# Linear attention: means' differences to GpSimd, halves added by a one-operand reduce, query dots ahead of the statistics

## The chip, the cores and the metric

The kernel runs on one core of a Trainium2 chip. Its engines work side by side, each through its own instructions in order: TensorE (PE, matrix products), VectorE (DVE), ScalarE (ACT), GpSimd (POOL) and SyncE (SP), which here only issues DMAs. They wait for one another on semaphores. The metric is the device time of one execution in microseconds; lower is better.

## The reference

A decoder layer in float32, on `x` and a context of 128 sequences of 64 positions and 128 features. Three steps follow one another, each on a layer norm of `x`, each added to `x`. The change touches the first alone:

```
b, t, e = x.shape                                  # 128, 64, 128; H = 16 heads of D = 8
q = feature_map(x @ wq + bq).reshape(b, t, H, D)   # where(x > 0, x + 1, exp(x))
k = feature_map(x @ wk + bk).reshape(b, t, H, D)
v = (x @ wv + bv).reshape(b, t, H, D)
# running over t:
S = S + einsum('bhd,bhe->bhde', kt, vt);  z = z + kt
num = einsum('bhd,bhde->bhe', qt, S);     den = einsum('bhd,bhd->bh', qt, z) + 1e-6
out = (num / den) @ wo + bo
```

`x` in it is layer-normed: `(x - mean) / sqrt(var + 1e-5)` over the 128 features. The second step is a cross attention by autocorrelation (softmax over the five best lags), the third a mixture of 8 experts, two for each row.

## The kernel before, in words

The 8192 rows are 64 tiles of 128 rows, and four tiles are a group, so there are 16 groups. The attention stage runs in slots n = -3 to 17. Each engine has its own function `slot(n, i)`; slots -3 to 3 are written out, slots 4 to 11 are a hardware loop of four rounds of two slots, slots 12 to 17 are written out again. In the loop, counts for semaphores are computed in registers. The order of the instructions in a slot is written by hand and differs between engines. One slot works on several groups at once: VectorE reads the statistics of the input of group n+3 (`z`), multiplies and sums group n (`b`), and divides and adds group n-1 (`c`); GpSimd makes features and outer products of group n+1; PE and ScalarE also prepare the Gram matrices of group n-2 (`d`).

In a slot VectorE does, for each tile k of group n, `times_q` (L908: R = running sums in PSUM times q) and `sum_heads` (L918: num = sum of R over d). Between them stand `inverses` (L957), `quotients` (L963, tile `on`), `stats` of the input (L884, four `bn_stats` into `st[:, 0]`), `key_dots` (L924: zq = key sums times q), `sum_dots` (L931), `add_attention` (L971, adds to X), `stats` of the new X (into `st[:, 1]`) and `moments` (L892, L893).

`bn_stats` gives six numbers for each row: count, mean and sum of squared deviations of the even elements, then the same three of the odd ones. `moments` makes two small tensors of them: `df`, the difference of the two means, and `mv`, the sum of the means and of the squared deviations. ScalarE (`deviations`, L679 and L680) squares `df` and scales `mv` into `sq` and `me`; GpSimd adds them (L534, `ve`), takes the power -0.5 (L542, `rs`), and makes the shift `nb` (L548, L551); ScalarE normalises rows with `rs` and `nb` (L685: `xh` for the attention, `xh2` for the Gram matrices).

GpSimd's slot is `root` (L534, L542), `features` of tile 0 (L560: qk = ex + rl, two tensors in SBUF), `shifts` (L548, L551), `outer_product` of tile 0 (L569), then features and outer product of tiles 1, 2 and 3. PE's slot has the running sums of the outer products (L1366, in the profile L1351 into `run`), the projections, the key sums (bank 4), the transposes of `on`, then `wkk` times `ct` into bank 4, which waits until `key_dots` has read that bank, then the output projection, the transposes of `xh2`, the running sums of tile 3, and the Gram matrices. Matrix products of all kinds have the line of the helper `mm`, L1351, and transposes L1355.

After the last slots the stored Gram matrices come back by DMA with another layout (`w_s<-gram_d`), and the cross attention starts by summing them (L1059).

Of the kernel before, what the change touches and what calls it, by code (L numbers as in the profile page):

```python
# [9 lines left out]
ALU = mybir.AluOpType  # L10
ACT = mybir.ActivationFunctionType
AX = mybir.AxisListType
# [6 lines left out]
GT = 4  # L19
# [36 lines left out]
def need(eng, sem, count):  # L56

    if not (isinstance(count, int) and count <= 0):
        eng.wait_ge(sem, count)
# [7 lines left out]
def build(nc, x, ctx_t, ctx_r, wqkv_p, b_all, wo, wq2, wk2, wv2t, wo2, bq2, bk2, bv2, scale, w_router, w_experts,  # L67
          tri, stri, ident, iota, dest, walk, place, late_in, out):
    with ExitStack() as ctx:
        def sb(name, shape, dt=F32):  # L70
            return ctx.enter_context(nc.sbuf_tensor(name, shape, dt))

        def sem(name):
            return ctx.enter_context(nc.semaphore(name))
# [49 lines left out]
        st = sb("st", [P, 2, GT, 6])  # L124
        mv, df = ([sb(f"{n}{i}", [P, 2, GT, w]) for i in range(2)] for n, w in (("mv", 2), ("df", 1)))
# [125 lines left out]
        x_in = sems("x_in", 2)  # L251
        ct_in = sems("ct_in", 2)

        m_st, m_mv, m_sq, m_ve, m_rs, m_mr, m_nb, a_xh = (sem(n) for n in ("m_st", "m_mv", "m_sq", "m_ve", "m_rs", "m_mr", "m_nb", "a_xh"))
        a_ex = sem("a_ex")
        a_tr, a_xT, a_proj, a_pev, a_f, a_outer = (sem(n) for n in ("a_tr", "a_xT", "a_proj", "a_pev", "a_f", "a_outer"))

# [40 lines left out]
        def settle(eng):  # L298


            eng.sem_inc(settled, 1)
# [19 lines left out]
        def stage(n, i, shift):  # L321

            if i is None and not 0 <= n + shift < NG:
                return None
            return grp(n + shift, i)

        def moment_slot(n, i, shift):

            at = n + shift if i is None else 2 * i + n + shift
            if i is not None:  # L330
                return at, (n + shift) % 2, slice(0, 2)
            if not -3 <= at <= NG:
                return None
            return at, at % 2, slice(0 if at + 3 < NG else 1, 2 if at >= 1 else 1)

        def stats_before(n, i):

            if i is not None:
                return 2 * GT * (2 * i + n + 1)
            return GT * (min(n + 3, NG) + min(max(n - 1, 0), NG))  # L340
# [176 lines left out]
        def _(pool):  # L517
# [9 lines left out]
            pool.memset(used[0][:], 0.0).then_inc(s_used, 1)  # L527
            pool.wait_ge(setup, 3)

            def root(at, p, own):  # L530

                pool.wait_ge(m_sq, 2 * (at + 3) + 2)
                need(pool, m_rs, at + 3)
                nc.gpsimd.tensor_tensor(ve[:, own], sq[:, own], me[:, own], ALU.add).then_inc(m_ve, 1)  # L534
                pool.wait_ge(m_ve, at + 4)
                if isinstance(at, int):
                    need(pool, a_xh, GT * min(at + 2, NG))
                    need(pool, d_xh, GT * (at - 2))
                else:
                    pool.wait_ge(a_xh, GT * (at + 2))  # L540
                    pool.wait_ge(d_xh, GT * (at - 2))
                nc.gpsimd.tensor_tensor(rs[p][:, own], ve[:, own], power[:, own], ALU.pow).then_inc(m_rs, 1)  # L542
# [19 lines left out]
            def outer_product(g, p, r, k):  # L562
                t = GT * g + k
                pool.wait_ge(a_f, t + 1)
                pool.wait_ge(a_pev, 3 * t + 3)
                need(pool, b_run, t - GT + 1)
                kk = qk[p][:, k, E:2 * E].rearrange("p (h d) -> p h d", h=H)
                vv = v8[k % 2][:].rearrange("p (h e) -> p h e", h=H)
                nc.gpsimd.tensor_tensor(  # L569
                    outer[k].rearrange("p (h e d) -> p h e d", h=H, e=D), vv.unsqueeze(3).broadcast_to([P, H, D, D]),  # L570
                    kk.unsqueeze(2).broadcast_to([P, H, D, D]), ALU.mult).then_inc(a_outer, 1)

            def slot(n, i):
                m, a1 = moment_slot(n, i, -1), stage(n, i, 1)
                if i is None and n == -1:
                    pool.wait_ge(bias_ch, 8)
                if m:
                    root(*m)
                if a1:
                    features(*a1, 0)  # L580
                if m:
                    shifts(*m)
                if a1:
                    outer_product(*a1, 0)
                    for k in range(1, GT):
                        features(*a1, k)
                        outer_product(*a1, k)

            slots(pool, slot)

            for k in range(2):
# [59 lines left out]
        def _(act):  # L651
# [22 lines left out]

            def deviations(at, p, own):

                act.wait_ge(m_mv, 2 * (at + 3) + 2)
                need(act, m_ve, at + 3)
                nc.scalar.activation(sq[:, own], df[p][:, own, :, 0], ACT.Square, scale=0.5).then_inc(m_sq, 1)  # L679
                nc.scalar.activation(me[:, own], mv[p][:, own, :, 1], ACT.Copy, bias=LN_EPS, scale=1.0 / E).then_inc(m_sq, 1)  # L680
# [161 lines left out]
        def _(dve):  # L842
# [35 lines left out]
                step(nc.vector.scalar_tensor_tensor(bias3[0:3, :], bias_p[2][:], id_s[0:3, 2:3], bias_r, ALU.mult, ALU.add))  # L878

            def stats(g, at, h):  # L880
                need(dve, m_mv, 2 * (at + 3))
                settle(dve)
                for k in range(GT):
                    nc.vector.bn_stats(st[:, h, k, :], X[:, bass.ds(GT * g + k, 1), :].rearrange("p a b -> p (a b)")  # L884
                                       ).then_inc(m_st, 1)

            def moments(at, p, own, seen):

                dve.wait_ge(m_st, seen)
                need(dve, m_mr, at + 2)  # L890
                settle(dve)
                nc.vector.tensor_tensor(df[p][:, own, :, 0], st[:, own, :, 1], st[:, own, :, 4], ALU.subtract).then_inc(m_mv, 1)  # L892
                nc.vector.tensor_tensor(mv[p][:, own], st[:, own, :, 1:3], st[:, own, :, 4:6], ALU.add).then_inc(m_mv, 1)  # L893

            def stats_e(g):
                need(dve, e_mv, GT * g)
# [24 lines left out]
            def key_dots(g, p, r):  # L921

                dve.wait_ge(b_keys, g + 1)
                nc.vector.tensor_tensor(  # L924
                    zq[:].rearrange("p (k c x) -> p c k x", k=GT, c=2), bank[4][:].rearrange("p (c k x) -> p c k x", c=2, k=GT),
                    qk[p][:, :, 0:E].rearrange("p k (c x) -> p c k x", c=2), ALU.mult).then_inc(b_dots, 1)
# [32 lines left out]
            def quotients(g, p, r):  # L959
                dve.wait_ge(c_rden, g + 1)  # L960
                need(dve, c_tr, g)
                dve.wait_ge(b_red, GT * g + GT)
                nc.vector.tensor_tensor(  # L963
                    on[:].rearrange("p t (h d) -> p (t h) d", h=H), num[p][:].rearrange("p t (h d) -> p (t h) d", h=H),
                    rden.unsqueeze(2).broadcast_to([P, GT * H, D]), ALU.mult).then_inc(c_on, 1)
# [8 lines left out]
            def slot(n, i):  # L974
                z, b, c, m = *(stage(n, i, k) for k in (3, 0, -1)), moment_slot(n, i, 0)
                if b:
                    times_q(*b, 0)
                    sum_heads(*b, 0)
                if c:
                    if i is None and c[0] == 0:  # L980
                        dve.wait_ge(kk_w, 1)
                    inverses(*c)
                if b:
                    times_q(*b, 1)
                if c:
                    quotients(*c)
                if z:
                    g, p, r = z
                    dve.wait_ge(x_in[p], 16 * r + 16)
                    stats(g, m[0], 0)  # L990
                if b:
                    key_dots(*b)
                if m and not c:
                    moments(*m, stats_before(n + 1, i))
                if b:
                    sum_heads(*b, 1)
                    sum_dots(*b)
                if i is None and n == -3:
                    fold_projection()
                    split_biases()  # L1000
                if i is None and n == -1:
                    dve.wait_ge(w_in, N_W)
                    nc.vector.tensor_copy(bv2_wide[:], bv2_s[:, 0:1].broadcast_to([P, P])).then_inc(fold_wide, 1)
                    fold_queries()
                if i is None and n == NG:
                    split_fold()
                if b:
                    times_q(*b, 2)
                    sum_heads(*b, 2)
                if c:  # L1010
                    add_attention(*c)
                if b:
                    times_q(*b, 3)
                if c:
                    dve.wait_ge(c_x1, c[0] + 1)
                    stats(c[0], m[0], 1)
                if b:
                    sum_heads(*b, 3)
                if c:
                    moments(*m, stats_before(n + 1, i))  # L1020
# [27 lines left out]
            n = 0  # L1048
# [146 lines left out]
            n = 0  # L1195
# [29 lines left out]
            for b in range(NT // NSORT):  # L1225
                own = slice(b * NSORT, (b + 1) * NSORT)
# [537 lines left out]
```

## Time and profile before

| | us |
|---|---|
| three timed runs | 618.99, 619.33, 620.18; median 619.33 |
| the profiled execution | 620.77 |
| its span, first to last instruction | 619.0 |
| the eight slots of the hardware loop (79.81 to 195.84) | 116.03 |
| VectorE busy in them | 114.61 |
| PE busy in them | 109.15 |
| GpSimd busy in them | 102.64 |
| ScalarE busy in them | 83.87 |
| ScalarE's waits for PE ahead of L664, nine slots | 10.8 |
| busy over the whole span: PE, VectorE, GpSimd, ScalarE | 554.9 (90%), 503.6 (81%), 410.3 (66%), 395.7 (64%) |

The attention stage takes the first 260 us or so of the span. Busy time counts an instruction from its start to its end, also the part in which it stands still. Instructions of one engine can overlap a little: the next one starts while the last one drains, so the time that an instruction takes from its engine is read from its start to the start of the next. An idle time in brackets behind a row names what ended it.

### The profile page before, as it was taken

What the parts mean: (1) busy time and instruction counts of PE and PEld (TensorE: products, weight loads), DVE (VectorE), ACT (ScalarE), POOL (GpSimd) and SP (SyncE); (2) the same over time, 40 slices, a digit from 0 to 9 for tenths busy, and PEclk for the clock granted to TensorE, in tenths of its full rate; (3) what the DMA queues carried; (4) which work ended last, traced back from release to release, by engine and by line L of the source; (5) the groups of instructions that cost most, each with busy time, mean ns of one, the idle gap of its engine ahead of it and who ended that gap; (6) DMA issues with size and microseconds to landing.
All of it is one profiled execution on the core that took longest, in us unless ns stands there. A gap on an engine that the chain in (4) does not pass through costs nothing.

```text
span 619.0 us, 16196 instructions
## 1 busy us (share of the span) xinstructions
PE 554.9 (90%) x4286; PEld 410.2 (66%) x4287; DVE 503.6 (81%) x1416; ACT 395.7 (64%) x1070; POOL 410.3 (66%) x475
## 2 busy tenths in 40 slices
PE   2888999999999998787998868999999999999993
PEld 1343444444444454465997535899999999999993
DVE  4499999999999999765487898466887878877883
ACT  3556777767666775423877412445888888878882
POOL 2999888888888985204876402764576766757762
PEclk9999999999999998989899887999999999999997
DMA  5510111111161111832566570221111111111110
GB/s 154 176 64 1 35 36 35 34 47 46 43 102 35 35 35 34 123 105 70 171 189 171 101 115 10 60 46 38 37 50 50 48 49 48 52 39 48 52 45 23
DMA packets 49976, 41.03 MB, mean 66 GB/s; under 512 B 21971, under 2 KB 40278, under 8 KB 49926
## 3 DMA queue, kind: packets, MB, share of 16 engines
q1 hardware_dynamic: 44150, 29.68, 19.8%
q0 software_dynamic: 4960, 10.49, 6.6%
q8 instruction: 23, 0.38, 0.3%
q10 hardware_dynamic: 816, 0.26, 0.2%
q14 instruction: 27, 0.22, 0.1%
HBM read 27.54 MB, written 12.88 MB: 65 GB/s over the span
## 4 chain that ended last, share of the span: by engine, by line
PE 54%; DVE 16%; issue 14%; DMA 5%; ACT 5%; POOL 4%; DVEq 1%; SPq 1%; POOLq 0%; ACTq 0%
PE bank L1351 28%; PE run L1351 22%; DVE st L884 3%; DVE R L908 3%; PE run L1618 2%; DMA w_s<-gram_d 2%; PE bank L1355 2%; ACT xs L788 2%; POOL qk L560 1%; DVE mean_early L1059 1%; DMA ct<-in_ctx_r 1%; ACT xh L685 1%; PE run L1542 1%; POOL shared L569 1%; DVE zq L924 1%
## 5 line engine op out<-in xcount | busy, mean ns | idle before, releaser
L569 POOL TENSOR_TENSOR shared<-v,qk 128x1024 f32<-128x1024 f32 x64 | 125.0, 1953 | 7.5 <-POOL qk L560 5.7
L624 POOL DMA_INDIRECT shared<-xs_d,row_u x91 | 87.7, 963 | 62.3 <-DVE row_u L1249 31.3
L631 POOL DMA_INDIRECT out_x<-shared x64 | 63.6, 994 | 47.6 <-DVE shared L1321 20.8
L908 DVE TENSOR_TENSOR R<-run,qk 128x1024 f32<-128x1024 f32 x64 | 77.7, 1215 | 10.5 <-PE run L1351 9.9
L918 DVE TENSOR_REDUCE num<-R 128x128 f32<-128x1024 f32 x64 | 77.7, 1213 | 1.5
L1351 PE MATMUL bank<-wqkv,xT 128*64 128x128 f32 (+1 forms) x384 | 69.9, 350 | 5.2 <-ACT v L667 4.5
L1351 PEld LDWEIGHTS bank<-wqkv,xT 128*64 128x64 f32 (+1 forms) x384 | 33.1, 158 | 59.0 <-issue 30.1
L1351 PE MATMUL run<-shared,tris_s 64*64 64x512 f32 x512 | 70.6, 622 | 0.1
L817 ACT ACTIVATE shared<-run,scale_s 128x128 f32<-128x128 f32 (+1 forms) x78 | 30.1, 386 | 41.2 <-PE run L1618 41.2
L685 ACT ACTIVATE xh<-X,nb,rs 128x128 f32 (+1 forms) x126 | 52.0, 502 | 4.4 <-POOL nb L551 4.4
L560 POOL TENSOR_TENSOR qk<-ex,rl 128x256 f32<-128x256 f32 x64 | 46.6, 728 | 9.1 <-ACT ex L669 6.9
L1351 PE MATMUL run<-w_s,hid 128*128 (+1 forms) x312 | 41.4, 275 | 0.0
L1351 PE MATMUL bank<-w_s,hid 128*128 (+1 forms) x308 | 41.0, 276 | 0.0
L821 ACT ACTIVATE ct<-w_s 128x512 f32 x64 | 39.7, 621 | 0.2 <-issue 0.2
L664 ACT ACTIVATE ex<-bank 128x256 f32<-128x256 f32 x64 | 24.5, 383 | 23.4 <-PE bank L1351 23.2
L706 ACT ACTIVATE oT<-bank 128x512 f32<-128x512 f32 x16 | 9.6, 597 | 46.7 <-PE bank L1355 46.7
L1342 DVE TENSOR_TENSOR hid<-run,shared 128x256 f32<-128x256 f32 x78 | 33.0, 423 | 7.6 <-ACT shared L827 7.4
L1351 PEld LDWEIGHTS run<-w_s,hid 128*128 128x128 f32 x312 | 38.1, 192 | 0.1
L1351 PEld LDWEIGHTS bank<-w_s,hid 128*128 128x128 f32 x308 | 37.6, 192 | 0.4 <-DVE hid L1342 0.2
L827 ACT ACTIVATE shared<-run 128x256 f32<-128x256 f32 x78 | 30.0, 385 | 11.1 <-PE run L1351 8.1
L827 ACT ACTIVATE shared<-bank 128x256 f32<-128x256 f32 x77 | 29.7, 386 | 10.5 <-PE bank L1351 8.2
L1342 DVE TENSOR_TENSOR hid<-bank,shared 128x256 f32<-128x256 f32 x77 | 32.5, 422 | 2.2 <-ACT shared L827 1.7
(271 smaller groups left out, 1417.0 us busy)
## 6 DMA issues: line engine op xcount, KB each, us to landing
xs_d<-xs SPq DMA_DIRECT2D x16, 270.0 KB, 5.4
X<-in_x SPq DMA_DIRECT2D x16, 256.0 KB, 2.8
ct<-in_ctx_t SPq DMA_DIRECT2D x16, 256.0 KB, 2.9
ct<-in_ctx_r SPq DMA_DIRECT2D x16, 256.0 KB, 3.7
gram_d<-gd SPq DMA_DIRECT2D x14, 256.0 KB, 2.4
w_s<-in_w_experts SPq DMA_DIRECT2D x8, 384.0 KB, 3.9
circ<-prob_d SPq DMA_DIRECT2D x30, 64.0 KB, 2.8
shared<-xs_d,row_u POOLq DMA_INDIRECT x91, 2.6
```

The source lines that it names most:

```text
L560: nc.gpsimd.tensor_tensor(qk[p][:, k, :], ex[k % 2][:], rl[k % 2][:], ALU.add).then_inc(a_f, 1)
L569: nc.gpsimd.tensor_tensor(outer[k].rearrange("p (h e d) -> p h e d", h=H, e=D), vv.unsqueeze(3).broadcast_to([P, H, D, D]), kk.unsqueeze(2 ...
L624: nc.gpsimd.indirect_dma_start(xg[q], None, xs_d[:, :], bass.IndirectOffsetOnAxis(ap=rows, axis=0)).then_inc(xg_in[q], 16)
L631: nc.gpsimd.indirect_dma_start(out[:, :], bass.IndirectOffsetOnAxis(ap=xg[(NXI + j) % NX][:, DEST:DEST + 1].bitcast(U32), axis=0), yg[q], ...
L685: nc.scalar.activation(dst[:, k, :], X[:, bass.ds(GT * g + k, 1), :].rearrange("p a b -> p (a b)"), ACT.Identity, bias=nb[p][:, h, k:k + 1 ...
L817: nc.scalar.activation(xgT[p][:, cols], bank[0][:, cols], ACT.Copy, scale=scale_s[:, 0:1]).then_inc(x_xT, 1)
L821: nc.scalar.activation(w_tile[n % 2][0], w_s[:, dyn(held[0] * W_E, 2 * HID)], ACT.Copy).then_inc(x_wa, 1)
L827: nc.scalar.activation(silu[p][h], bank[1 + 2 * p + h][:, HID:2 * HID], ACT.Silu).then_inc(x_silu, 2 // len(items_of(i, up[0])))
L908: nc.vector.tensor_tensor(R[:, 0:D * E].rearrange("p (h e d) -> p h e d", h=H, e=D), run[k % 2][:].rearrange("p (h e d) -> p h e d", h=H, ...
L918: nc.vector.tensor_reduce(num[p][:, k, :], R[:, 0:D * E].rearrange("p (x d) -> p x d", d=D), AX.X, ALU.add).then_inc(b_red, 1)
L1342: nc.vector.tensor_tensor(hid[p][h][:], bank[1 + 2 * p + h][:, 0:HID], silu[p][h], ALU.mult).then_inc(x_h, 2 // len(items_of(i, j)))
L1351: return nc.tensor.matmul(o, l, r, start=start, stop=stop, skip_group_check=True)
```

## The change

`df` is made on GpSimd by a new function `differences`, which stands between `features` and `outer_product` of tile 3 and signals on a new semaphore `m_df`. `mv` stays on VectorE, but is a `tensor_reduce` over the two halves of `st`, seen as the last axis: one operand of 32 elements a partition instead of two of 16. In VectorE's slot `key_dots` comes before `stats` of the input. ScalarE's `deviations` waits for `m_df` and `m_mv`, and `stats` waits for both before it writes `st` again.

```diff
+            def differences(at, p, own, seen):
+
+                pool.wait_ge(m_st, seen)
+                need(pool, m_sq, 2 * (at + 2))
+                nc.gpsimd.tensor_tensor(df[p][:, own, :, 0], st[:, own, :, 1], st[:, own, :, 4], ALU.subtract).then_inc(m_df, 1)
...
             def slot(n, i):
-                m, a1 = moment_slot(n, i, -1), stage(n, i, 1)
+                m, now, a1 = moment_slot(n, i, -1), moment_slot(n, i, 0), stage(n, i, 1)
...
                 if a1:
                     outer_product(*a1, 0)
-                    for k in range(1, GT):
+                    for k in range(1, GT - 1):
                         features(*a1, k)
                         outer_product(*a1, k)
+                    features(*a1, GT - 1)
+                if now:
+                    differences(*now, stats_before(n + 1, i))
+                if a1:
+                    outer_product(*a1, GT - 1)
...
             def deviations(at, p, own):
 
-                act.wait_ge(m_mv, 2 * (at + 3) + 2)
+                act.wait_ge(m_df, at + 4)
+                act.wait_ge(m_mv, at + 4)
                 need(act, m_ve, at + 3)
...
             def stats(g, at, h):
-                need(dve, m_mv, 2 * (at + 3))
+                need(dve, m_mv, at + 3)
+                need(dve, m_df, at + 3)
                 settle(dve)
...
-                nc.vector.tensor_tensor(df[p][:, own, :, 0], st[:, own, :, 1], st[:, own, :, 4], ALU.subtract).then_inc(m_mv, 1)
-                nc.vector.tensor_tensor(mv[p][:, own], st[:, own, :, 1:3], st[:, own, :, 4:6], ALU.add).then_inc(m_mv, 1)
+                halves = st[:, own].rearrange("p s t (h f) -> p s t f h", h=2)[:, :, :, 1:3]
+                nc.vector.tensor_reduce(mv[p][:, own], halves, AX.X, ALU.add).then_inc(m_mv, 1)
...
                 if c:
                     quotients(*c)
+                if b:
+                    key_dots(*b)
                 if z:
                     g, p, r = z
                     dve.wait_ge(x_in[p], 16 * r + 16)
                     stats(g, m[0], 0)
-                if b:
-                    key_dots(*b)
```

## Rows read from the trace of the kernel before

**Rows 1.** Windows: busy time of each engine over the loop's eight slots.
```profile
sum 116.03, PE 109.15 PEld 53.29 DVE 114.61 ACT 83.87 POOL 102.64; mean PE 13.64 PEld 6.66 DVE 14.33 ACT 10.48 POOL 12.83
```

**Rows 2.** Windows: slots 13 and 14, and the sum of slots 2, 3, 12, 13, 14.
```profile
210.21:224.38 14.17, 13.80 (x107) 6.66 (x99) 13.59 (x20) 10.31 (x33) 12.82 (x12) 1.00 0.13 39
224.38:238.12 13.74, 13.10 (x99) 6.24 (x95) 13.16 (x22) 8.64 (x28) 12.15 (x12) 1.00 0.14 39
sum 70.94, PE 65.72 PEld 32.38 DVE 69.03 ACT 49.93 POOL 63.44; mean PE 13.14 PEld 6.48 DVE 13.81 ACT 9.99 POOL 12.69
```

**Rows 3.** Timeline of VectorE in the loop: start us, us, line, operation [idle before].
```profile
156.93 0.86 DVE L884 BATCH_NORM_STATS2 st<-X 128x6 f32 x4
157.72 0.67 DVE L924 TENSOR_TENSOR zq<-bank,qk 128x512 f32<-128x512 f32 x1
...
162.41 0.68 DVE L971 TENSOR_TENSOR X<-X,bank 128x512 f32 x1
163.15 1.23 DVE L908 TENSOR_TENSOR R<-run,qk 128x1024 f32<-128x1024 f32 x1
...
166.19 0.63 DVE L892 TENSOR_TENSOR df<-st 128x8 f32<-128x8 f32 x1
166.74 0.16 DVE L893 TENSOR_TENSOR mv<-st 128x16 f32<-128x16 f32 x1
166.83 1.21 DVE L908 TENSOR_TENSOR R<-run,qk 128x1024 f32<-128x1024 f32 x1
```

**Rows 4.** Timeline of GpSimd in the loop: tile 0's features, then tile 3.
```profile
156.63 0.73 POOL L560 TENSOR_TENSOR qk<-ex,rl 128x256 f32<-128x256 f32 x1
157.31 0.20 POOL L548 TENSOR_TENSOR mr<-mv,rs 128x8 f32<-128x8 f32 x1
...
166.07 0.72 POOL L560 TENSOR_TENSOR qk<-ex,rl 128x256 f32<-128x256 f32 x1 [0.25 <-ACT ex L669]
167.02 1.95 POOL L569 TENSOR_TENSOR shared<-v,qk 128x1024 f32<-128x1024 f32 x1 [0.23 <-POOL qk L560]
```

**Rows 5.** Timeline of slot 1, VectorE and GpSimd at the moments.
```profile
50.41 0.16 DVE L892 TENSOR_TENSOR df<-st 128x8 f32<-128x8 f32 x1
50.49 0.73 DVE L893 TENSOR_TENSOR mv<-st 128x16 f32<-128x16 f32 x1
...
50.41 0.78 POOL L560 TENSOR_TENSOR qk<-ex,rl 128x256 f32<-128x256 f32 x1
```

**Rows 6.** Waits from 79 to 209 us (nine slots): us in total, times, longest.
```profile
PE bank L1351 <- DVE zq L924: 6.0, 9, 0.7
...
POOL qk L560 <- ACT ex L669: 2.7, 9, 0.5
...
POOL qk L560 <- POOL shared L569: 1.8, 9, 0.2
```

**Rows 7.** Groups of instructions in the loop: count | busy us, mean ns | idle before.
```profile
L918 DVE TENSOR_REDUCE num<-R 128x128 f32<-128x1024 f32 x32 | 38.8, 1213 | 0.9
...
L931 DVE TENSOR_REDUCE den<-zq 128x64 f32<-128x512 f32 x8 | 5.4, 676 | 0.0
```

**Rows 8.** Timeline of PE: slots of the loop, then slots 13 and 14.
```profile
161.41 0.66 PE L1355 MATMUL bank<-id_s,xh 128*128 128x128 f32 x4
...
170.43 1.09 PE L1351 MATMUL run<-shared,tris_s 64*64 64x512 f32 x8
...
214.99 0.63 PE L1355 MATMUL bank<-id_s,on 128*128 128x128 f32 x4
...
218.84 0.66 PE L1355 MATMUL bank<-id_s,xh 128*128 128x128 f32 x4 [0.24 <-ACT xh L685]
...
229.17 0.63 PE L1355 MATMUL bank<-id_s,on 128*128 128x128 f32 x4 [0.40 <-DVE on L963]
```

**Rows 9.** Timeline of VectorE at the end of the attention stage.
```profile
261.69 0.83 DVE L1043 TENSOR_SCALAR xh<-X,rs,nb 128x128 f32<-128x128 f32 x2 [1.69 <-POOL nb L551]
262.70 7.15 DVE L1059 TENSOR_REDUCE mean_early<-w_s 112x64 f32<-112x4096 f32 x1 [0.19 <-DMA w_s<-gram_d]
```

More of the change, by code:

```diff
@@ L252, in build @@
         ct_in = sems("ct_in", 2)
-        m_st, m_mv, m_sq, m_ve, m_rs, m_mr, m_nb, a_xh = (sem(n) for n in ("m_st", "m_mv", "m_sq", "m_ve", "m_rs", "m_mr", "m_nb", "a_xh"))
+        m_st, m_mv, m_df, m_sq, m_ve, m_rs, m_mr, m_nb, a_xh = (sem(n) for n in ("m_st", "m_mv", "m_df", "m_sq", "m_ve", "m_rs", "m_mr", "m_nb", "a_xh"))
         a_ex = sem("a_ex")
```

## The prediction
> **What bounds the kernel now.** I read the page first. Over the whole span no engine is full (PE is busy for 90%, VectorE for 81%), but the change sits in the attention stage only, so I cut that stage into slots with the windows view, from one product `R` of tile 0 (L908) to the next. The eight slots of the hardware loop take 116.03 us, 14.50 each, and VectorE is busy for 114.61 of them, 99% [rows 1]. The slots written out around the loop take 13.7 to 14.4 us [rows 2]. So VectorE sets the pace, but PE (109.15) and GpSimd (102.64, without its short gaps) are close behind, and what the change gives ends where one of them takes over.
>
> Busy is not the same as working. In the timeline `df` (L892), a subtraction of 8 elements per partition, lasts 0.63 us, and `mv`, which adds twice as many, 0.16 [rows 3]. GpSimd's `qk` (L560) runs from 166.07 to 166.79, and `df` ends at 166.82 [rows 4]: the end of one is the end of the other. At slot 1 `qk` runs 50.41 to 51.19; there `df` got through in 0.16 and it is `mv` that lasts 0.73, to 51.22 [rows 5]. Both are VectorE instructions with two operands in SBUF, and so is `qk` on GpSimd. The wait is not for data, it is for GpSimd's instruction to end. `R` (L908), with one operand in PSUM, runs beside GpSimd at its usual 1.21. The Trainium skill says the same in "SBUF — State Buffer", section "Who interferes with whom": a VectorE instruction with two SBUF inputs and a GpSimd instruction that reads SBUF exclude each other, and `tensor_reduce` on trn2 never takes part. This case's trace agrees on the first half (0.63 against 0.16), and on the second as far as reduces of 1024 elements go.
>
> A second wait is PE's: it waits 6.0 us in 9 slots for `zq` (L924), 0.67 each, before it multiplies `ct` by `wkk` [rows 6]. PE works in order, so that wait is handed on to the running sums of tile 3. VectorE feels its tail: `X` starts at 162.41 and ends at 163.09, and `R` of tile 3 starts only at 163.15, where `R` after `mv` starts 0.07 before `mv` ends [rows 3]. That is some 0.15 us per slot.
>
> **The change part by part, for one slot of the loop.**
>
> *`df` leaves VectorE.* From `df`'s start to `mv`'s is 0.55 us (166.19 to 166.74) [rows 3]. All of it goes: -0.55.
>
> *`mv` becomes a reduce.* It reads 32 elements instead of two operands of 16. No row shows so small a reduce; the two that there are take 1213 ns for 1024 elements and 676 ns for 512 [rows 7], which is 1.05 ns an element and 0.14 fixed, so 0.17 for 32. The ends are 0.16 (`mv` now) and 0.68 (the smaller reduce, if its time were mostly fixed, which would eat nearly all of the 0.55). I take 0.18, by the line through both rows: +0.02. If a reduce were held up by GpSimd as `mv` was, the stall would stay; the reduces of 1024 ran beside GpSimd all the time with a mean of 1213 ns [rows 7], which speaks against it.
>
> *`zq` moves ahead of the statistics.* It starts 0.79 earlier (157.72 to 156.93) and the four `bn_stats` one `zq` later, about 0.6 [rows 3]. PE's 0.67 of waiting goes, of which some 0.35 reach tile 3's sums: the transposes of `xh2` need ScalarE's normalised rows, and in slot 13, where PE doesn't wait for `zq`, it waits 0.24 for those rows instead [rows 8]. VectorE's 0.15 goes. The later statistics are read only at the end of the slot, 9 us on. No DMA is issued in the moved step, and nothing is moved past in SP's or GpSimd's queue; SP's context load follows `d_k`, which comes earlier.
>
> *`df` on GpSimd.* It stands between `qk` and `outer` of tile 3. These start 0.95 apart with `qk` 0.72 long, so 0.23 is a gap for the semaphore [rows 4]. A tensor_tensor of the same size, `mr`, starts 0.68 after its `qk` and takes 0.20 [rows 4], so `df` would be over after 0.88, inside the 0.95. The two new waits compare with register values. Their cost isn't shown by itself: at least 0, at most one more gap like the 0.23 plus `df`'s own 0.20, 0.43 in all. I take 0.03. Behind it in GpSimd's queue stand `outer` of tile 3, then `ve` and `rs` of the next slot.
>
> *ScalarE waits for both `df` and `mv`.* `df` is over some 0.1 later than now. Behind that wait is the evacuation of projection 0 (L664), and it waits for PE anyway, 10.8 us in nine slots by the waits view. If that cover were gone it would cost 0.1.
>
> *Waits before the statistics* (`m_df` beside `m_mv`): `df` will have been read behind `qk` of tile 3, at some 152.5 for the statistics at 157.5; nothing.
>
> **What is late next.** Three floors for a slot of the loop:
> - VectorE: 14.50 - 0.55 + 0.02 - 0.15 = 13.82.
> - GpSimd: of its 14.50, 2.7 + 1.8 us in 9 slots are waits ahead of `qk` for ScalarE's `ex`, which come of phase [rows 6]; that leaves 14.50 - 0.50 + 0.03 = 14.03.
> - PE and ScalarE in turn: transposes of `on` to those of the rows, 3.85 where `zq` isn't waited for (214.99 to 218.84), then from the rows' transposes to the end of tile 2's sums, 161.41 to 171.52, 10.11 [rows 8]. Sum 13.96.
>
> GpSimd has microseconds of lead over most of its readers, so 8 slots of 0.07 more than PE hardly show. I take 14.0: 0.50 saved per slot, 8 x 0.50 = 4.0.
>
> Outside the loop: slots 2, 3 and 12 take 70.94 - 14.17 - 13.74 = 43.03, 14.34 each [rows 2]; GpSimd's gaps are shorter there and VectorE's floor of 13.82 holds: 3 x 0.5 = 1.5. Slot 1 has a stall of 0.57 (0.73 against 0.16) with PE waiting: 0.6. Slot 13 has no statistics between `on` and `zq`, so the move does nothing, but its stall goes; PE waited 0.40 for the `on` that followed [rows 8], and that is what comes through: 0.4. Slot 14 is bound by PE: 0.1. At the end the last group's `df` is now a step on GpSimd between VectorE and ScalarE, 0.1 to 0.2 longer. VectorE waits 1.69 for `nb` there and then 0.19 for a DMA [rows 9], so at most 0.1 comes through. Sum: 4.0 + 1.5 + 0.6 + 0.4 + 0.1 - 0.1 = 6.5 us. Everything behind the attention hangs on its last Gram store, and I let it move up as a block.
>
> The profiled execution took 620.77 us around a span of 619.0. So the profiled one becomes 614.3 with a span of 612.5, and as the timed runs have a median of 619.33, the median becomes 612.8.
>
> **Rivals.**
> - *PE and ScalarE, or GpSimd, bind earlier* (chance 0.20). The floors are sums of single links; if the ring of PE and ScalarE keeps some of its short waits, or `df` on GpSimd costs its upper 0.43, a slot of the loop is 14.2 to 14.4. For: all three floors are within 0.2 of each other, and VectorE lost by 0.55 + 0.15 what the other two have not. Against: slot 14, bound by PE, takes 13.74. It gives 8 x 0.2 + 1.5 + 0.6 = 3.7 us: 615.6.
> - *VectorE alone sets the pace* (0.08): 8 x 0.68 instead of 4.0 makes 7.9: 611.4.
> - *The stall passes to the reduce, or the reduce is long* (0.06). Then only the 0.15 of the moved dots comes through, 1.2 us at the most, partly lost: 618.8. The 0.73 of `mv` in slot 1 shows that a stall can pass on; the 1213 of the reduces speaks against.
> - *Slower: `df` on GpSimd is held up in its turn* (0.06). Place: between `qk` and `outer` of tile 3, where VectorE now starts `R` at the very time. If GpSimd had to let `R` (1.21) end, the pair would be 0.95 + 1.0 or so apart, GpSimd's slot 14.0 + 1.0 = 15.0, against 14.50: +4.0 in the loop, less 1.1 still won outside it: 622.2. It decides from 0.5 us on per slot. Against: GpSimd's `outer` starts at 167.02 in the middle of an `R` and lasts its 1.95 [rows 3, 4]. By the same page of the Trainium skill an instruction with at most one SBUF input doesn't contend, so this would not happen; the trace agrees.
>
> **How the numbers follow.** My forecast has 0.60, with its own range 611.7 to 614.3. Less than 0.2% (1.24 us) can't be told from no change. Faster: 0.60 + 0.20 + 0.08, and a little of the fourth case, 0.89; same 0.05; slower 0.06. The range takes in the two neighbours, 611.0 to 616.4, and leaves out both the passed-on stall and the slower case.
>
> **What would show it.** The `df` group on POOL with a mean near 0.2 us, and `outer` of tile 3 still 0.95 after its `qk`. A reduce for `mv` of 0.15 to 0.2 in all its instances. PE's wait for `zq` gone; VectorE's `R` of tile 3 without a wait; VectorE's busy share in the loop below 99%, with short waits for PE or GpSimd. Slots of 14.0 us and a Gram store of the last part some 6 us earlier. A slot of 14.3 or more, with VectorE waiting for `run`, would refute the floors of PE and GpSimd; a long `mv` refutes the cause of the stall.

## The result, and the profile after

The changed kernel takes 611.85 us (median of 4 runs, 611.06 to 613.12), the kernel before in the same comparison 619.50. The ratio is 0.9878, with a 95% interval of 0.9858 to 0.9897: 7.65 us between the medians. A second comparison (`changed_again` below) gave 612.97 against 618.74, a ratio of 0.9908 (0.9881 to 0.9936), 5.8 us. The forecast was 612.8, 6.5 us below the kernel before. The profiled execution took 611.89 us around a span of 610.1.

The same windows as in [rows 1], the eight slots of the loop, now from 79.15 to 190.48 us (us of the window, busy time and instructions of PE, PEld, DVE, ACT, POOL, granted clock, DMA share, GB/s):

```profile
120.98:134.86 13.88, 13.45 (x103) 6.65 (x99) 13.79 (x22) 10.38 (x34) 12.90 (x14) 1.00 0.13 38
134.86:148.84 13.98, 13.56 (x103) 6.61 (x99) 13.78 (x23) 10.33 (x34) 12.99 (x14) 1.00 0.13 38
...
sum 111.33, PE 107.93 PEld 53.10 DVE 110.21 ACT 82.61 POOL 103.06; mean PE 13.49 PEld 6.64 DVE 13.78 ACT 10.33 POOL 12.88
```

111.33 instead of 116.03: 13.92 us a slot, 4.7 saved. VectorE's timeline in the loop of the changed kernel, to be held against [rows 3]:

```profile
139.52 0.68 DVE L937 TENSOR_TENSOR zq<-bank,qk 128x512 f32<-128x512 f32 x1
140.12 0.86 DVE L897 BATCH_NORM_STATS2 st<-X 128x6 f32 x4
...
145.00 0.68 DVE L984 TENSOR_TENSOR X<-X,bank 128x512 f32 x1
145.59 1.22 DVE L921 TENSOR_TENSOR R<-run,qk 128x1024 f32<-128x1024 f32 x1
...
148.63 0.17 DVE L906 TENSOR_REDUCE mv<-st 128x16 f32<-128x32 f32 x1
148.84 1.23 DVE L921 TENSOR_TENSOR R<-run,qk 128x1024 f32<-128x1024 f32 x1
```

The long `df` is gone and `mv` takes 0.17. `R` of tile 3 starts 0.59 after `X`, no longer 0.74. But from `mv`'s start to `R`'s it is 0.21 here, and was 0.09. GpSimd's timeline at the same place, against [rows 4]:

```profile
148.68 0.73 POOL L566 TENSOR_TENSOR qk<-ex,rl 128x256 f32<-128x256 f32 x1
149.37 0.21 POOL L534 TENSOR_TENSOR df<-st 128x8 f32<-128x8 f32 x1
149.64 1.95 POOL L575 TENSOR_TENSOR shared<-v,qk 128x1024 f32<-128x1024 f32 x1
```

`outer` starts 0.96 after its `qk`, as before with nothing between them. And the waits in nine slots, against [rows 6] (us in total, times, longest):

```profile
ACT ex L675 <- PE bank L1364: 8.7, 10, 1.0
...
PE bank L1368 <- ACT xh L697: 3.3, 9, 0.5
...
ACT sq L691 <- POOL df L534: 1.6, 7, 0.3
POOL qk L566 <- ACT ex L680: 0.7, 2, 0.4
```

PE's 6.0 us for `zq` are gone. In their place PE waits 3.3 for ScalarE's normalised rows (`xh2`, written by L697). ScalarE waits 1.6 for `df` (L691), and behind that still 8.7 for PE (L675). GpSimd's waits for `ex` fell from 2.7 to 0.7.

Where the time went, by landmarks on VectorE (starts of the first `R` of a slot, and of the first sum of the cross attention):

| stretch | before | after | difference |
|---|---|---|---|
| start to slot 0 | 24.83 | 24.67 | -0.2 |
| slot 0 | 11.91 | 13.00 | +1.1 |
| slot 1 | 14.41 | 13.79 | -0.6 |
| slots 2, 3, 12 | 43.03 | 41.48 | -1.5 |
| slots 4 to 11 (loop) | 116.03 | 111.33 | -4.7 |
| slots 13 and 14 | 27.91 | 27.37 | -0.5 |
| slot 15 to `mean_early` | 24.58 | 24.41 | -0.2 |
| up to `mean_early` | 262.70 | 256.05 | -6.65 |
| behind it, to the end of the span | 356.3 | 354.05 | -2.2 |

The last line is no effect of the change that I can show. The same code behind the attention stage took 352.8 to 357.0 us in the profiled executions of the variants below, and 355.8 in the changed kernel's second. The landmark of 256.05 came back at 256.04, but its first and last stretch scatter, too: over all traces the start of slot 0 lies at 24.26 to 24.83, and the stretch from slot 15 to `mean_early` takes 23.39 to 24.58, with 24.19 and 23.39 in two traces of one and the same kernel (`slot0_order` and `slot0_again`). What the change does is best read from slots 0 to 14 alone: 213.29 us before, 206.97 after and 207.05 in the changed kernel's second trace. That is 6.3 us.

### The profile page after: what moved, and what is told of

Same layout as the page of the kernel before. It is cut to its first block, busy times and chain, and to the rows that moved or that the text cites. A ratio compares the mean times of both kernels' runs of the same rounds, so it can differ in the third digit from the quotient of the medians.

```text
span 610.1 us, 16245 instructions
## 1 busy us (share of the span) xinstructions
PE 553.6 (91%) x4286; PEld 409.2 (67%) x4287; DVE 496.9 (81%) x1396; ACT 394.2 (65%) x1070; POOL 413.5 (68%) x495
## 4 chain that ended last, share of the span: by engine, by line
PE 44%; issue 19%; POOL 13%; DVE 11%; DMA 5%; ACT 5%; SPq 2%; POOLq 1%; DVEq 0%; ACTq 0%
PE bank L1364 21%; PE run L1364 20%; POOL shared L575 5%; POOL qk L566 4%; DMA X<-in_x 3%; ACT xs L800 2%; PE run L1631 2%; DMA shared<-xs_d,row_u 1%; SPq L420 1%; DVE mean_early L1072 1%; ACT xh L697 1%; PE run L1555 1%; DVE R L921 1%; PE bank L1368 1%; DVE st_e L911 1%
## 5 line engine op out<-in xcount | busy, mean ns | idle before, releaser
L697 ACT ACTIVATE xh<-X,nb,rs 128x128 f32 (+1 forms) x126 | 52.3, 510 | 4.5 <-POOL nb L557 4.3
L675 ACT ACTIVATE ex<-bank 128x256 f32<-128x256 f32 x64 | 24.8, 388 | 18.6 <-PE bank L1364 18.5
```

The costliest lines, as they stand in the source:

```text
L697: nc.scalar.activation(dst[:, k, :], X[:, bass.ds(GT * g + k, 1), :].rearrange("p a b -> p (a b)"), ACT.Identity, bias=nb[p][:, h, k:k + 1 ...
```

## The experiments

Each was timed in five rounds beside the kernel before, in three jobs; a number in brackets is the interval of the ratio. The table gives from each one's trace the mean loop slot, the sum of slots 0 to 14 (before 213.29, changed 206.97) and the landmark `mean_early`.

| kernel | us (before in that job) | ratio | loop slot | slots 0 to 14 | mean_early |
|---|---|---|---|---|---|
| dots_only | 620.77 (617.86) | 1.005 (1.003 to 1.0071) | 14.42 | 215.40 | 263.97 |
| dots_back | 613.80 (617.86) | 0.9941 (0.9918 to 0.9963) | 14.07 | 207.96 | 255.91 |
| two_operands | 617.23 (617.86) | 0.9992 (0.997 to 1.0013) | 13.91 | 212.23 | 261.03 |
| reduce_only | 618.55 (617.86) | 1.0012 (0.9994 to 1.0031) | 14.50 | 213.10 | 261.50 |
| slot0_order | 612.11 (617.52) | 0.9903 (0.9868 to 0.9938) | 13.92 | 205.83 | 254.36 |
| pool_extra | 612.47 (617.52) | 0.992 (0.9891 to 0.9948) | 13.92 | 206.53 | 255.02 |
| dve_extra | 613.47 (617.52) | 0.9934 (0.9908 to 0.996) | 13.99 | 208.19 | 256.26 |
| act_extra | 616.07 (617.52) | 0.9977 (0.9955 to 0.9999) | 14.19 | 210.99 | 259.79 |
| changed_again | 612.97 (618.74) | 0.9908 (0.9881 to 0.9936) | 13.92 | 207.05 | 256.04 |
| slot0_again | 610.14 (618.74) | 0.986 (0.9837 to 0.9884) | 13.91 | 206.08 | 253.90 |
| pool_larger | 612.18 (618.74) | 0.9908 (0.9872 to 0.9944) | 14.03 | 207.99 | 256.19 |

**The parts one at a time.** `dots_only`: the kernel before, with

```diff
                 if c:
                     quotients(*c)
+                if b:
+                    key_dots(*b)
                 if z:
...
-                if b:
-                    key_dots(*b)
```

> The kernel before with one edit: the dots of q stand in front of the input's statistics; df and mv stay on VectorE as two-operand instructions. Main theory (the stall comes of two SBUF operands on VectorE meeting GpSimd's qk, the move only takes PE's wait for zq away): df still lasts about 0.6 us, R of tile 3 loses its 0.15 us of waiting, a loop slot goes from 14.50 to about 14.35, and slot 0 costs 0.9 us, since zq waits there 0.7 for the key sums that the statistics covered. Together -0.5 to -1.5 us: 618 to 619. Rival (the moved dots are the main gain, because PE's wait of 0.67 per slot holds everybody): loop slots near 13.9 and 613 or less.

Slower than before by 0.5%, where 0.5 to 1.5 us less were expected. The loop slot came out at 14.42 (14.35 was expected), but slots 0 and 1 took 29.54 us (14.15 and 15.39) instead of 26.32: `df` met GpSimd's `outer` there and lasted 1.70 and 1.71 us. In the loop `R` of tile 3 does start 0.59 to 0.60 after `X`, so the 0.15 is gone, but the stall has grown by some 0.07, and it now goes to and fro. VectorE's timeline of two slots, and GpSimd's features of tile 3 beside them:

```profile
139.23 0.68 DVE L892 TENSOR_TENSOR df<-st 128x8 f32<-128x8 f32 x1
139.84 0.16 DVE L893 TENSOR_TENSOR mv<-st 128x16 f32<-128x16 f32 x1
153.67 0.16 DVE L892 TENSOR_TENSOR df<-st 128x8 f32<-128x8 f32 x1
153.75 0.74 DVE L893 TENSOR_TENSOR mv<-st 128x16 f32<-128x16 f32 x1
...
139.16 0.72 POOL L560 TENSOR_TENSOR qk<-ex,rl 128x256 f32<-128x256 f32 x1 [0.25 <-ACT ex L669]
...
153.68 0.77 POOL L560 TENSOR_TENSOR qk<-ex,rl 128x256 f32<-128x256 f32 x1 [0.25 <-ACT ex L669]
```

In the first slot `qk` has begun, and `df` waits for its end. In the second `df` is 0.01 ahead of `qk` and gets through in 0.16, `qk` is 0.05 longer than usual, and it is `mv` behind it that waits until `qk` ends. Who comes first goes first; the two slots alternate like this through the whole loop.

`reduce_only`: the kernel before with `mv` as the one-operand reduce (the two lines of the change's diff), `df` left where it was.

> The kernel before with one edit: mv is the one-operand reduce; df stays on VectorE with its two operands, the dots stay behind the statistics. Main theory: df still lasts 0.6 in the loop, mv 0.18; only slot 1, where mv had the stall, can gain 0.5 at most: 619 to 620. Rival (a lighter mv also lets df through): 615 or less.

As the main theory had it: loop slots of 14.50, `df` 0.62 to 0.63 in them, `mv` 0.15 to 0.18 everywhere, and the time that of before. In slot 1 the stall, which `mv` had before, is now on `df` (0.53), and the slot is 0.19 shorter. A light `mv` does nothing for a `df` that meets GpSimd.

`dots_back`: the changed kernel with the dots behind the statistics.

> The changed kernel with one edit undone: the dots of q stand behind the input's statistics again; df on GpSimd and the one-operand reduce stay. Main theory: no stall, PE waits for zq again. A loop slot 14.0 to 14.1, slot 0 gains 0.9 us back: 612 to 613.5, close to the changed kernel. Rival (both edits are needed together, PE's wait for zq caps the slot as soon as VectorE is faster): loop slots of 14.3 and more, 616 or more.

The loop slot is 14.07, 0.15 more than in the changed kernel. PE waits 4.4 us in nine slots for `zq`, and `R` of tile 3 again starts 0.74 after `X`. Slot 0 is 1.2 us shorter (11.83 against 13.00). Over slots 0 to 14 this kernel takes 207.96 against 206.97: the move gives back 2.2 us in the later slots, pays 1.2 of them in slot 0, and is worth 1.0 in all. That `mean_early` comes at the same time (255.91) is due to the two stretches that scatter. By the times it is 613.8 and 0.9941, and the changed kernel's two ratios are 0.9878 and 0.9908, from other jobs; I don't read a difference from that.

`two_operands`: the changed kernel with `mv` as it was,

```diff
-                halves = st[:, own].rearrange("p s t (h f) -> p s t f h", h=2)[:, :, :, 1:3]
-                nc.vector.tensor_reduce(mv[p][:, own], halves, AX.X, ALU.add).then_inc(m_mv, 1)
+                nc.vector.tensor_tensor(mv[p][:, own], st[:, own, :, 1:3], st[:, own, :, 4:6], ALU.add).then_inc(m_mv, 1)
```

> The changed kernel with one edit undone: mv is again a tensor_tensor with two SBUF operands, on VectorE; df stays on GpSimd, the dots stay in front. Main theory: mv now meets GpSimd's qk, df or outer product and lasts until it ends, 0.3 to 0.8 us in most slots instead of 0.16; the slot goes back to 14.2 to 14.5 and the time to 615 to 618. Rival (the gain is that one instruction less stands on VectorE, whatever its operands): mv 0.16 in all slots and the time that of the changed kernel, 612.

The time was in the expected range, the way there was not. In the loop `mv` takes 0.17 to 0.19 with both operands in SBUF, and the slots are as short as the changed kernel's, 13.91. The whole loss is outside it, where `mv` lasts 1.71 in slot 0, 1.76 in slot 1, 0.54 in slots 2 and 3, 0.57 and 0.70 in 12 and 13. Against the changed kernel slot 0 is 2.4 us longer, slot 1 1.6, and these four 0.2 to 0.5 each. VectorE and GpSimd in slots 0 and 1, then in the loop:

```profile
31.46 1.71 DVE L905 TENSOR_TENSOR mv<-st 128x8 f32<-128x8 f32 x1 [0.18 <-DVE st L897]
...
53.50 1.76 DVE L905 TENSOR_TENSOR mv<-st 128x16 f32<-128x16 f32 x1
...
152.87 0.17 DVE L905 TENSOR_TENSOR mv<-st 128x16 f32<-128x16 f32 x1
...
31.20 1.95 POOL L575 TENSOR_TENSOR shared<-v,qk 128x1024 f32<-128x1024 f32 x1
...
53.28 1.96 POOL L575 TENSOR_TENSOR shared<-v,qk 128x1024 f32<-128x1024 f32 x1
...
152.99 0.73 POOL L566 TENSOR_TENSOR qk<-ex,rl 128x256 f32<-128x256 f32 x1
```

31.46 + 1.71 = 33.17, and `outer` ends at 33.15; 53.50 + 1.76 = 55.26, and `outer` ends at 55.24. In the loop slot shown `mv` has started 0.12 before `qk` and is nearly through; in an earlier one it starts only 0.02 before `qk` (97.17 and 97.19) and still takes 0.17. So the reduce is worth its 5.3 us (212.23 to 206.97 over slots 0 to 14) not in the steady loop but where VectorE and GpSimd stand in another phase, that is, where the one comes to `mv` while the other is in the middle of an instruction. As a reduce `mv` takes 0.16 to 0.18 in every slot of every trace that has `df` on GpSimd, whatever the phase.

**Slot 0.** `slot0_order` and `slot0_again` are the same kernel, the changed one with the old order in slot 0:

```diff
+                early = i is None and n == 0
-                if b:
+                if b and not early:
                     key_dots(*b)
                 if z:
...
+                if b and early:
+                    key_dots(*b)
```

> The changed kernel, but in slot 0 alone the statistics stand in front of the dots of q as before. In the changed kernel zq waits 0.73 us there for the key sums and mv 0.18 for the statistics. Main theory: both waits go and the rest moves up, 0.9 us less: 611.0. Rival (another engine sets slots 0 and 1, or the time is lost again later): same as the changed kernel within 0.3.

> The changed kernel with the old order of dots and statistics in slot 0 alone, a second time, now beside the changed kernel on one chip. Its first trace had the attention stage end 1.7 us earlier than the changed kernel's. Expected: 1 to 2 us below the changed kernel; rival (lost again in the later stages): equal to it.

`changed_again` stood beside the second:

> The changed kernel itself, unedited, so that it stands beside the others on one chip. Main theory: its attention stage ends 6.6 us earlier than before, and the rest of its gain of 7.6 in the first comparison lay in the later stages, where executions differ from one another by a microsecond or two: -5.5 to -7.5 against before. Rival (the change also makes the later stages 1 us faster): -7.6 and a shorter stretch behind the attention stage again.

In the changed kernel `zq` waits in slot 0 for key sums that PE has just begun, and `mv` waits for statistics that nothing covers; with the old order both waits are gone:

```profile
29.19 0.69 DVE L937 TENSOR_TENSOR zq<-bank,qk 128x512 f32<-128x512 f32 x1 [0.73 <-PE bank L1364]
...
30.84 0.17 DVE L906 TENSOR_REDUCE mv<-st 128x8 f32<-128x16 f32 x1 [0.18 <-DVE st L897]
```

```profile
28.33 0.86 DVE L897 BATCH_NORM_STATS2 st<-X 128x6 f32<-128x128 f32 x4
29.14 0.69 DVE L937 TENSOR_TENSOR zq<-bank,qk 128x512 f32<-128x512 f32 x1
29.75 0.16 DVE L906 TENSOR_REDUCE mv<-st 128x8 f32<-128x16 f32 x1
```

(the first is the changed kernel, the second `slot0_again`). Slot 0 takes 11.84 and 12.13 us in the two traces, against 13.00 and 13.10 in the changed kernel's two and 11.91 before, and no other slot up to 14 differs by more than 0.02. Slot 0 scatters a little itself: in `pool_larger` and `dve_extra`, which leave it as it is in the changed kernel, it takes 12.79 and 12.89. So the old order is worth about 1 us there, near the 0.9 that was expected. `mean_early` comes 1.7 and 2.1 earlier, but what goes beyond 1.1 lies in the stretches that scatter. In one job the medians are 610.14 against 612.97, and 8.6 us (1.4%) below the kernel before. Of these 2.8 us only about 1 is shown to come of the edit: in its first job the same kernel had the ratio 0.9903, no better than the changed kernel's 0.9878 and 0.9908.

**What sets the slot of 13.92.** `act_extra`: one more copy on ScalarE ahead of the normalised rows `xh2`.

```diff
+                    nc.scalar.activation(dx[:], wqkv[:, 0:2 * E], ACT.Copy).then_inc(m_dx, 1)
                     norm(g, m[0], m[1], 1, xh2, d_xh, GT // 2 if i is None and g == NG - 1 else GT)
```

> The changed kernel with one more copy on ScalarE in front of the normalised rows for the Gram matrices (128x256 of a constant weight tile into a tile that nobody reads), about 0.3 us in every slot with that step (14 to 16 of them). PE waits 0.4 per slot for those rows in the changed kernel. If the ring of PE and ScalarE sets the slot: +0.25 per slot, +3 to +4 us. If VectorE or GpSimd set it with the ring 0.1 behind: +2. If ScalarE has room: within 0.3.

ScalarE in the loop:

```profile
143.71 0.44 ACT L728 ACTIVATE dx<-wqkv 128x256 f32<-128x256 f32 x1
144.02 1.65 ACT L699 ACTIVATE xh<-X,nb,rs 128x128 f32 x4
```

The copy takes 0.31 of ScalarE's time (from its start to that of `xh`), and the loop slot grows by 0.27 (113.50 for the eight). So the ring of PE and ScalarE (PE waits for ScalarE's rows, ScalarE for PE's products) stood only 0.04 below the slot of 13.92.

`dve_extra`: one more reduce on VectorE behind `mv`.

```diff
+                    nc.vector.tensor_reduce(dx[:, 0:H], wqkv[:, 0:E].rearrange("p (h d) -> p h d", h=H), AX.X, ALU.add).then_inc(m_dx, 1)
```

> The changed kernel with one more reduce on VectorE behind mv (128 elements of a constant weight tile to 16, into a tile that nobody reads, in slots 1 to 16), 0.28 us by itself, about 0.2 of VectorE's time. If VectorE sets the slot of 13.9 (its floor was forecast at 13.82, and its timeline shows no gap in the loop): +0.2 per slot, 13 or so slots, +2.5 us. If PE and ScalarE or GpSimd set it with VectorE 0.1 behind: +1.3. If VectorE has room: 0.

VectorE in the loop:

```profile
135.05 0.18 DVE L908 TENSOR_REDUCE mv<-st 128x16 f32<-128x32 f32 x1
135.14 0.28 DVE L912 TENSOR_REDUCE dx<-wqkv 128x16 f32<-128x128 f32 x1
135.34 1.22 DVE L927 TENSOR_TENSOR R<-run,qk 128x1024 f32<-128x1024 f32 x1
```

From `mv` to `R` it is 0.29, only 0.08 more than the 0.21 without the reduce, and the slot grows by 0.08 (111.95 for the eight). In the written-out slots, where it was 0.12 without, the slot grows by 0.17. Less time was added than expected, but all of it reaches the slot, so VectorE is at its floor, too.

`pool_extra` and `pool_larger` put a tensor_tensor behind `df` on GpSimd, of 8 and of 128 elements.

> The changed kernel with one more small tensor_tensor on GpSimd behind df (a sum of two constant operands of df's size into a tile that nobody reads). The gap behind qk is filled by df, so this one costs GpSimd 0.2 to 0.3 us per slot. If GpSimd is one of the engines that set the slot of 13.9: loop slots 14.1 to 14.2, +2 us in all, less in the written-out slots where GpSimd has 0.5 to spare. If it isn't: within 0.3 of the changed kernel.

> The changed kernel with a larger tensor_tensor on GpSimd behind df in slots 1 to 16 (128x128 of a constant weight tile into a tile that nobody reads), some 0.45 us, of which the gap behind qk hides nothing more. The small one tried before cost GpSimd only 0.05 per slot and moved nothing, so it could not tell. If GpSimd stands at its floor in the loop (13.9 by its own timeline): loop slots +0.35 to +0.4, 114 to 114.5 us for the eight. If it has room against PE and ScalarE, the slots grow by that much less; by 0 if it has 0.4.

```diff
+                nc.gpsimd.tensor_tensor(dx[:, own, :, 0], power[:, own], power[:, own], ALU.add).then_inc(m_dx, 1)      # pool_extra
...
+                    nc.gpsimd.tensor_tensor(dx[:, 0:E], wqkv[:, 0:E], wqkv[:, E:2 * E], ALU.add).then_inc(m_dx, 1)      # pool_larger
```

Two slots of `pool_larger` by the windows view, slot 4 and slot 9:

```profile
78.76:92.73 13.97, 13.46 (x103) 6.64 (x99) 13.78 (x22) 10.21 (x33) 13.04 (x15) 1.00 0.14 40
...
148.53:162.71 14.18, 13.32 (x103) 6.45 (x100) 13.87 (x22) 10.41 (x33) 13.26 (x15) 1.00 0.13 37
```

The small one moved `outer` by 0.05 and nothing else: no answer. The larger one moved it by 0.31. Of the eight loop slots the first four stay at 13.88 to 13.97, then come 14.07, 14.18, 14.20 and 14.09; the eight take 112.24, less than the 114 that was expected. GpSimd's `df` in the first of them shows why:

```profile
93.23 0.21 POOL L536 TENSOR_TENSOR df<-st 128x8 f32<-128x8 f32 x1
...
107.42 0.21 POOL L536 TENSOR_TENSOR df<-st 128x8 f32<-128x8 f32 x1
...
121.61 0.21 POOL L536 TENSOR_TENSOR df<-st 128x8 f32<-128x8 f32 x1
```

Here it already comes every 14.19 us, while VectorE's slots still take 13.88 and 13.97. GpSimd runs ahead of its readers, falls 0.26 behind in each slot, and only when the lead is used up does its own slot become everybody's. 14.19 less the 0.31 is 13.88, and that is, by this reckoning, GpSimd's floor in the changed kernel.

## Why the prediction was right, step by step

- *`df` leaves VectorE, -0.55, because two SBUF operands meet GpSimd.* Shown. `dots_only` and `two_operands` move the stall to `mv` and to other GpSimd instructions, and each time it ends 0.02 to 0.04 after that instruction. With `df` on GpSimd and `mv` a reduce no trace has it.
- *The reduce is never held up and costs +0.02.* Both hold: 0.16 to 0.18 in all 20, and from its start to `R`'s it is 0.10 in `reduce_only`'s loop and 0.12 in the changed kernel's written-out slots, where the sum has 0.11. What the sum lacks is another term. In the changed kernel's loop 0.21 pass until `R`, and in `two_operands`, where `mv` is no reduce, it is 0.20 to 0.22 as well: it is not the reduce. The extra reduce of `dve_extra` added only 0.08 there and not 0.2, so about 0.1 of the 0.21 is a delay of `R` that other work on VectorE can cover, as `df`'s stall did. What the loop's slots have and the written-out ones don't are counts computed in registers; that these are the cause is argued, not shown. So VectorE's floor is 13.92, not 13.82.
- *The moved dots take away 0.15 on VectorE and give PE 0.35.* In the loop, yes: `dots_back` is 0.15 slower per slot, `R` of tile 3 starts 0.74 after `X` there and 0.59 with the move, and PE now waits 0.37 for ScalarE's rows. That the 0.67 would not all come through was right.
- *`df` on GpSimd is free.* In the loop, yes: `outer` 0.96 after `qk`, was 0.95. In the written-out slots it costs 0.05 (0.85 after `qk`, was 0.80).
- *ScalarE's wait for both costs nothing.* It waits 1.6 us for `df`, and the cover is there: 8.7 us of waiting for PE behind it.
- *Floors of 13.82, 14.03 and 13.96, slot 14.0.* Measured: floors of 13.92, 13.88 and 13.88, slot 13.92. VectorE's was taken 0.1 too low, GpSimd's 0.15 and the ring's 0.1 too high. The forecast let GpSimd and PE set the slot, and it is VectorE that does. That 14.0 came so near 13.92 is in part luck: the three errors don't point the same way. 4.7 were saved, not 4.0.
- *Slots 2, 3, 12: 1.5.* Measured 1.55. *Slots 13 and 14: 0.4 + 0.1.* Measured 0.54, all of it in slot 13.
- *Slot 1: 0.6.* Measured 0.62.
- *Slot 0.* It has no term in the sum, and that is the worst error: it lost 1.1 us. I looked at the moved dots in the loop, where the key sums end 1.7 us before `zq` starts (137.79 and 139.52), and never asked in slot 0, where they are not ready. `slot0_order` and `slot0_again` show that order as the cause: with the old one slot 0 is back at 11.8 and 12.1.
- *The rest moves up as a block, at most 0.1 lost.* The stage's end moved by 6.65 where 6.5 was the sum, and slots 0 to 14 by 6.3 where it has 6.6. The nearness is partly luck: the loop gave 0.7 more than its term, slot 0 took 1.1 that had none.

Of the rivals, none came. The slower one, GpSimd's `df` held up by `R`, is refuted by its 0.20 to 0.21 us in every slot, with `R` running beside it. The Trainium skill, "SBUF — State Buffer", section "Who interferes with whom", says of the shared ports that issue order decides who blocks; the trace of `dots_only` agrees, with 0.01 us between the two outcomes.

## What to carry to other kernels

A tiny instruction with a long duration is standing still: compare its end with the ends on the other engine, and change its operands or its engine, so that what it meets no longer matters. When an instruction is moved ahead of another that filled the time until its data came, ask in every kind of slot, the first above all, whether what it reads is ready. And before a gain is counted, add up the floors of the other engines; here three of them lay within 0.1 us. Here 0.55 and 0.15 were taken from the busiest, and 0.59 came through, because the stall had covered another delay of 0.1.

## What the runs showed of the hardware

That a stall can pass on to the next instruction by 0.01 us was new to me, and that one of 8 elements can take 1.7 us: it lasts until 0.02 to 0.04 us after the end of the GpSimd instruction that it meets. GpSimd's `qk` lost only 0.05 (0.77 or 0.78 for 0.73) when VectorE was first by 0.01 to 0.02.
